# State space layer of a decoder: two states on the two halves of the partitions, sums by 64-column matmuls, and one scan per item in every chunk

## The reference

```python
proj = xc @ W_xproj                      # dt_r (16), Bm (16), Cm (16)
dt = softplus(dt_r @ W_dt + b_dt)        # (b, t, 512)
dA  = exp(dt[..., None] * -exp(A_log))   # (b, t, 512, 16)
dBx = (dt * xc)[..., None] * Bm[:, :, None, :]
h_t = h_{t-1} * dA_t + dBx_t             # from h = 0 for each of 4 sequences
y_t = sum over n of h_t[..., n] * C_t[n]
y = (y + xc * D) * silu(z);  out = x + y @ W_out
```

## Time and profile before

| | |
|---|---|
| median of 3 runs (lowest, highest) | 3203.89 us (3202.26, 3206.14) |
| the profiled execution: its own time, its span | 3204.56 us, 3203.0 us |
| busy over the span | PE 2843.9, DVE 2080.0, POOL 1509.9, ACT 1471.0 us |
| the state space stage | 0 to about 1013 us of the span |
| first scan; first scan of chunk 2 | 40.07 us; 291.29 us |
| mean granted TensorE clock of the whole span | 0.957 |

### The profile page before, as it was taken

The page is one execution under the profiler, slowest core; times in us unless marked ns, Lnnn a source line. Parts: engine busy times, 40 slices in busy tenths (PEclk is TensorE's granted clock), DMA queues, the critical chain, the costliest instruction groups (busy, mean ns, idle before and its releaser), DMA issues. The chain is left out here.

```text
span 3203.0 us, 41427 instructions
## 1 busy us (share of the span) xinstructions
PE 2843.9 (89%) x14210; PEld 1845.6 (58%) x14210; DVE 2080.0 (65%) x3833; ACT 1471.0 (46%) x2768; POOL 1509.9 (47%) x1192
## 2 busy tenths in 40 slices
PE   6898998998977877899999999978877999999998
PEld 2343343343333664555555555546666888888887
DVE  7899999999998654677777777758863222222221
ACT  5667667666763301366666656545541111111111
POOL 5788788888785553133333333256752111111111
PEclk8999999999999788899999999999888999999999
DMA  7135145145140162212322222110115665556662
GB/s 233 51 108 159 46 116 160 35 125 159 34 136 1 41 211 94 81 42 65 81 63 65 58 50 64 50 59 29 50 63 198 200 203 183 181 181 187 205 199 60
DMA packets 283856, 346.32 MB, mean 108 GB/s; under 512 B 85788, under 2 KB 238552, under 8 KB 283592
## 3 DMA queue, kind: packets, MB, share of 16 engines
q1 hardware_dynamic: 260399, 310.17, 31.3%
q0 software_dynamic: 16704, 27.21, 3.6%
q10 hardware_dynamic: 6544, 6.30, 0.7%
HBM read 234.69 MB, written 107.95 MB: 107 GB/s over the span
## 5 line engine op out<-in xcount | busy, mean ns | idle before, releaser
L542 POOL TENSOR_TENSOR mb_drive<-mb_dtx,mb_b_rep 128x1024 f32<-128x1024 f32 x255 | 597.0, 2355 | 179.9 <-DVE mb_pD L439 87.9
L853 PE MATMUL mb_pY<-mb_hc,ident 128*128 128x512 f32 x1024 | 502.9, 616 | 55.9 <-DVE mb_hc L456 55.5
L1981 DVE TENSOR_REDUCE at_nm_of<-at_pS 128x1 f32<-128x128 f32 (+1 forms) x756 | 401.6, 556 | 135.8 <-PE at_pS L1969 75.8
L3153 POOL DMA_INDIRECT out<-et_y,et_to x71 | 112.0, 1577 | 667.0 <-DVE et_y L3207 411.0
L3197 DVE TENSOR_TENSOR et_mT<-et_silu,et_pU 128x512 f32<-128x512 f32 (+1 forms) x160 | 100.3, 628 | 471.2 <-ACT et_silu L3168 471.1
L3168 ACT ACTIVATE et_silu<-et_pG 128x512 f32<-128x512 f32 (+1 forms) x160 | 87.8, 549 | 658.0 <-PE et_pU L3229 658.0
L853 PEld LDWEIGHTS mb_pY<-mb_hc,ident 128*128 128x128 f32 x1024 | 190.3, 195 | 326.9 <-issue 183.3
L1969 PE MATMUL at_pS<-at_kT,at_qT 128*128 128x128 f32 (+1 forms) x756 | 306.3, 407 | 65.3 <-DVE at_nm_of L1981 53.4
L598 ACT ACTIVATE mb_pD<-mb_dt,mb_a_neg 128x512 f32<-128x512 f32 x384 | 259.6, 688 | 157.3 <-DVE mb_hc L456 146.0
L439 DVE TENSOR_TENSOR_SCAN mb_pD<-mb_pD,mb_drive 128x1024 f32<-128x1024 f32 x128 | 292.7, 2287 | 42.9 <-ACT mb_pD L596 40.2
L445 DVE TENSOR_TENSOR_SCAN mb_pD<-mb_pD,mb_carried,mb_drive 128x512 f32<-128x512 f32 x256 | 314.0, 1271 | 6.8 <-ACT mb_pD L598 6.8
(11 more groups left out here) (491 smaller groups left out, 4984.7 us busy)
## 6 DMA issues: line engine op xcount, KB each, us to landing
t_wg<-in_t_wgT SPq DMA_DIRECT2D x40, 1024.0 KB, 6.3
t_wu<-in_t_wuT SPq DMA_DIRECT2D x40, 1024.0 KB, 8.8
t_wd<-in_t_wdT SPq DMA_DIRECT2D x40, 1024.0 KB, 11.3
mb_b_rep<-mb_rows SPq DMA_DIRECT2D x64, 512.0 KB, 5.6
mb_c_rep<-mb_rows SPq DMA_DIRECT2D x64, 512.0 KB, 4.8
t_h_sorted<-blank SPq DMA_DIRECT2D x6, 4160.0 KB, 20.2
t_h_sorted<-blank SPq DMA_DIRECT2D x18, 1170.0 KB, 6.2
t_h_sorted<-blank SPq DMA_DIRECT2D x12, 1040.0 KB, 5.8
```

The costliest lines, as they stand in the source:

```text
L542: nc.gpsimd.tensor_tensor(drive[G % RINGS][:, :, :], dtx[:, m, :].unsqueeze(1).to_broadcast([P, 2, CH]), b_rep[:, 2 * j:2 * j + 2, :], ALU ...
L853: last = nc.tensor.matmul(pY[:, :], K.ident[:, :], hc[G % RINGS][:, k, :], start=False, stop=(j == PAIRS - 1 and k == 1))
L1981: nc.vector.tensor_reduce(nm_of[t % 2][:, w0 // 512, a, qb:qb + 1], score_bank(t, k)[:, 0:w1 - w0], axis=AX.X, op=ALU.max, negate=True).th ...
```

## The change

Two states now lie on the two halves of the partitions (`h`), and two halves of a channel block on the two halves of the free dimension (`k`): `pD[r][h*64 + p, k, t]` is state 2j+h of channel k*64+p. So `b_rep` and `c_rep` have 8 rows to a partition in place of 16 and are loaded by two DMAs of 64 partitions (128 KB) each, for each of b and c. `dt` and `dtx` must be seen by both halves: eight SBUF to SBUF DMAs of 128 KB for each block (`twins`) write them into `dt2` and `dtx2`, which have `TWINS` = 3 slots, and all decays and drives read these. `A_log` is laid out so on the host. The sum over the two states is a matmul with `fold` (two identities of 64 under each other, 64 columns), one for each half of the channels into its 64 partitions of `pY`. In odd chunks there is one scan of 1024 as well: its start is the first carried value, the decay in front of the second half is 0, and ACT adds decay times the second carried value to the first element of the second half's drive. The decays of these first elements come from one more small activation per block (`opening`). `step_sizes` of the next chunk's block 0 comes before drive 29 in place of 31.

```diff
+    TWINS = 3
-        a_neg = sb("a_neg", [P, ME, NST])
+        a_neg = sb("a_neg", [P, ME, 2, PAIRS])
+        fold = sb("fold", [P, HP])
-        b_rep, c_rep = sb("b_rep", [P, NST, CH]), sb("c_rep", [P, NST, CH])
+        dt2, dtx2 = sb("dt2", [P, TWINS, 2, CH]), sb("dtx2", [P, TWINS, 2, CH])
+        b_rep, c_rep = sb("b_rep", [P, PAIRS, CH]), sb("c_rep", [P, PAIRS, CH])
...
+            def twins(ch, m):
+                nth = ch * ME + m
+                q = nth % TWINS
+                for made, to, s_made, s_to, s_used, per in ((dt, dt2, s_dt, s_dt2, s_dec, 2), (dtx, dtx2, s_dtx, s_dtx2, s_drv, 1)):
+                    eng.wait_ge(s_made, nth + 1)
+                    if nth >= TWINS:
+                        eng.wait_ge(s_used, (nth - TWINS + 1) * PAIRS * per)
+                    for k in range(2):
+                        for h in range(2):
+                            eng.dma_start(to[h * HP:(h + 1) * HP, q, k, :], made[k * HP:(k + 1) * HP, m, :]).then_inc(s_to[q], 16)
...
                     if ch > 0:
                         eng.wait_ge(s_drv, last_user + 1)
-                    eng.dma_start(b_rep[:, 2 * j:2 * j + 2, :], rows_dram[ch % 2][2 * j:2 * j + 2, :].partition_broadcast(P)).then_inc(s_b[j], 16)
+                    for h in range(2):
+                        eng.dma_start(b_rep[h * HP:(h + 1) * HP, j, :], rows_dram[ch % 2][2 * j + h, :].partition_broadcast(HP)).then_inc(s_b[j], 16)
                     if ch > 0:
                         eng.wait_ge(s_hc, last_user + 1)
-                    eng.dma_start(c_rep[:, 2 * j:2 * j + 2, :],
-                                  rows_dram[ch % 2][NST + 2 * j:NST + 2 * j + 2, :].partition_broadcast(P)).then_inc(s_c[j], 16)
+                    for h in range(2):
+                        eng.dma_start(c_rep[h * HP:(h + 1) * HP, j, :], rows_dram[ch % 2][NST + 2 * j + h, :].partition_broadcast(HP)).then_inc(s_c[j], 16)
+                    if j == 5:
+                        twins(ch, 0)
                 fill_rows(K, eng, K.h1_sorted, ch, NCH, s_fill)
+                for m in range(1, ME):
+                    twins(ch, m)
...
+        def drive_of(unit, ch, m, j, r):
+            return unit.tensor_tensor(drive[r][:, :, :], dtx2[:, (ch * ME + m) % TWINS, :, :],
+                                      b_rep[:, j, :].unsqueeze(1).to_broadcast([P, 2, CH]), ALU.mult)
...
+                if ch % 2 and G % ITEMS in (0, RINGS):
                     eng.wait_ge(s_keep, ch // 2 * ITEMS + (ITEMS - RINGS if G % ITEMS == 0 else ITEMS))
-                for k in range(2):
-                    eng.wait_ge(s_dec, 2 * G + k + 1)
-                    nc.vector.tensor_tensor_scan(pD[r][:, k, :], pD[r][:, k, :], drive[r][:, k, :],
-                                                 carried[:, m, 2 * j + k:2 * j + k + 1], ALU.mult, ALU.add).then_inc(s_scan, 1)
+                eng.wait_ge(s_dec, 2 * G + 2)
+                both = lambda T: T[r][:, :, :].rearrange("p k t -> p (k t)")
+                before = carried[:, m, j, 0:1] if ch % 2 else 0.0
+                nc.vector.tensor_tensor_scan(both(pD), both(pD), both(drive), before, ALU.mult, ALU.add).then_inc(s_scan, 2)
...
-                    eng.wait_ge(s_dtx, ch * ME + m + 1)
+                    twin_made(eng, s_dtx2, ch * ME + m)
...
-                    if s == 31 and ch + 1 < NCH:
+                    if s == 29 and ch + 1 < NCH:
                         step_sizes(eng, nc.gpsimd, ch + 1, 0)
...
+                nc.scalar.activation(pD[r][:, 1, 1:], step[:, 1:], ACT.Exp, scale=scale)
+                blank = nc.scalar.copy(pD[r][:, 1, 0:1], zeros[:, 0:1])
+                if ch % 2 == 0:
+                    blank.then_inc(s_dec, 1)
+                    return
+                eng.wait_ge(s_opening, ch // 2 * ME + m + 1)
+                eng.wait_ge(s_keep, ch // 2 * ITEMS + G % ITEMS + 1)
+                eng.wait_ge(s_drv, G + 1)
+                nc.scalar.activation(drive[r][:, 1, 0:1], opening[:, m, j:j + 1], ACT.Identity, scale=carried[:, m, j, 1:2],
+                                     bias=drive[r][:, 1, 0:1]).then_inc(s_dec, 1)
...
-                    nc.tensor.matmul(pY[:, :], skip[:, m, :], xc(ch, m), start=True, stop=False)
+                    for k in range(2):
+                        nc.tensor.matmul(pY[k * HP:(k + 1) * HP, :], skip[:, m, k * HP:(k + 1) * HP], xc(ch, m), start=True, stop=False,
+                                         skip_group_check=True)
...
-                    last = nc.tensor.matmul(pY[:, :], K.ident[:, :], hc[G % RINGS][:, k, :], start=False, stop=(j == PAIRS - 1 and k == 1))
+                    last = nc.tensor.matmul(pY[k * HP:(k + 1) * HP, :], fold[:, :], hc[G % RINGS][:, k, :], start=False, stop=(j == PAIRS - 1),
+                                            skip_group_check=True)
```

More of the change, by code:

```diff
@@ L226, in mamba @@
     PAIRS = NST // 2
+    HP = P // 2
+    TWINS = 3
     ITEMS = ME * PAIRS
@@ L288, in mamba @@
             sem(n) for n in ("dec", "drv", "scan", "keep", "hc", "y", "fin", "rows", "fill"))
+        s_dt2, s_dtx2 = [sem(f"dt2_{q}") for q in range(TWINS)], [sem(f"dtx2_{q}") for q in range(TWINS)]
+        s_fold = sem("fold")
+        s_opening = sem("opening")
         s_b = [sem(f"b{j}") for j in range(PAIRS)]
@@ L349, in _, with twin_made @@
             for j in range(PAIRS):
-                eng.wait_ge(s_b[j], 16 * NCH)
-                eng.wait_ge(s_c[j], 16 * NCH)
-        ALL_IN = 16 * 7
+                eng.wait_ge(s_b[j], 32 * NCH)
+                eng.wait_ge(s_c[j], 32 * NCH)
+            for q in range(TWINS):
+                uses = len(range(q, NCH * ME, TWINS))
+                eng.wait_ge(s_dt2[q], 64 * uses)
+                eng.wait_ge(s_dtx2[q], 64 * uses)
+        ALL_IN = 16 * 7
+        def twin_made(eng, s_to, nth):
+            eng.wait_ge(s_to[nth % TWINS], 64 * (nth // TWINS + 1))
+        def drive_of(unit, ch, m, j, r):
+            return unit.tensor_tensor(drive[r][:, :, :], dtx2[:, (ch * ME + m) % TWINS, :, :],
+                                      b_rep[:, j, :].unsqueeze(1).to_broadcast([P, 2, CH]), ALU.mult)
         def normalise(eng, unit, ch):
@@ L426, in first_drive @@
             def first_drive():
[L427 to L430, removed]
+                twin_made(eng, s_dtx2, 0)
+                eng.wait_ge(s_b[0], 32)
+                drive_of(nc.vector, 0, 0, 0, 0).then_inc(s_drv, 1)
             def scans(G):
@@ L470, in _ @@
             nc.vector.memset(K.start.before[:, :], 1.0).then_inc(s_set, 1)
+            nc.vector.tensor_tensor(fold[:, :], K.ident[:, 0:HP], K.ident[:, HP:P], ALU.add).then_inc(s_fold, 1)
             eng.wait_ge(s_cw, 16)
@@ L577, in keep @@
                 eng.wait_ge(s_hc, G + 1)
-                nc.scalar.copy(carried[:, m, 2 * j:2 * j + 2], pD[G % RINGS][:, :, CH - 1]).then_inc(s_keep, 1)
+                nc.scalar.copy(carried[:, m, j, :], pD[G % RINGS][:, :, CH - 1]).then_inc(s_keep, 1)
             def decay(G, k):
@@ L582, in decay @@
                 r = G % RINGS
-                scale = a_neg[:, m, 2 * j + k:2 * j + k + 1]
+                scale = a_neg[:, m, k, j:j + 1]
+                step = dt2[:, (ch * ME + m) % TWINS, k, :]
                 if k == 0:
                     if j == 0:
-                        eng.wait_ge(s_dt, ch * ME + m + 1)
+                        twin_made(eng, s_dt2, ch * ME + m)
                     if G == RINGS - 1:
@@ L593, in decay @@
                             eng.wait_ge(s_keep, back // 2 * ITEMS + (G - RINGS) % ITEMS + 1)
-                if k == 1 and ch % 2 == 0:
-                    nc.scalar.activation(pD[r][:, 1, 1:], dt[:, m, 1:], ACT.Exp, scale=scale)
-                    nc.scalar.copy(pD[r][:, 1, 0:1], zeros[:, 0:1]).then_inc(s_dec, 1)
-                else:
-                    nc.scalar.activation(pD[r][:, k, :], dt[:, m, :], ACT.Exp, scale=scale).then_inc(s_dec, 1)
+                if k == 0:
+                    nc.scalar.activation(pD[r][:, 0, :], step, ACT.Exp, scale=scale).then_inc(s_dec, 1)
+                    if j == 0 and ch % 2:
+                        nc.scalar.activation(opening[:, m, :], a_neg[:, m, 1, :], ACT.Exp,
+                                             scale=dt2[:, (ch * ME + m) % TWINS, 1, 0:1]).then_inc(s_opening, 1)
+                    return
[3 more added lines that the diff above has]
+                    blank.then_inc(s_dec, 1)
+                    return
+                eng.wait_ge(s_opening, ch // 2 * ME + m + 1)
[3 more added lines that the diff above has]
+                                     bias=drive[r][:, 1, 0:1]).then_inc(s_dec, 1)
             def transposed(ch, k):
@@ L749, in _ @@
             projected(0)
-            nc.scalar.activation(a_neg[:, :, :], a_neg[:, :, :], ACT.Exp).then_inc(s_a, 1)
+            nc.scalar.activation(a_neg[:, :, :, :], a_neg[:, :, :, :], ACT.Exp).then_inc(s_a, 1)
             for m in range(2):
```

34 lines of the change are left out of this document (17 added, 17 removed).

## The result

The changed kernel takes 3301.21 us (median of 4 runs, 3296.75 to 3308.99), against 3203.07 us for the kernel before (median of 4, 3202.26 to 3206.14). The ratio is 1.0307, 95% interval 1.0286 to 1.0328: 98 us slower, where 70 were predicted, and inside the range of 3225 to 3314. The profiled execution of the changed kernel has a span of 3298.2 us (3203.0 before).

A forecast was written before the change was run, and what follows sets the result against it. DVE was taken to set the pace, the others having little to spare. Terms -21.5 - 14 + 40 + 12 + 16 + 21 + 12 + 8.5 - 4 = +70 gave 3274 us, range 3225 to 3314.

The forecast's parts named there:

- The copies behind t = 0: Chunk boundary: copies issued only after item 29's weigh ends (t = 0) delay the next chunk's first drive; +40 us, bounds 27 to 49.
- The start: Chunk 0: SP issues 24 half loads before block 0's copies, delaying the first decay and drive; +8.5 us, bounds 4 and 13.
- POOL's lost lead: After the late first drive, POOL runs without a break and drive 3 comes late; +12 us, bounds 0 and 20.
- the fill: Block 1's copies stand behind `fill_rows` on SP, making drive 9 late; +16 us, bounds 0 and 56.
- rival C: The fill holds block 1's copies fully, 56 us in place of 16: 3314 us; chance 0.10.
- Step sizes before drive 29: Chunk end: drive 29 waits behind step sizes that wait for ACT's logarithm; +21 us, bounds 5 and 30.
- both decays: Odd chunks: one scan waits for both of ACT's decays, where the first could start after one; +12 us, bounds 0 and 20.
- The scans: Odd chunks: 128 items go from a period of 3.49 to 3.32 us; -21.5 us.
- The sums: PE's two column groups overlap, cutting DVE's direct and indirect waits for PE; -14 us, bounds 0 and -30.
- B: Only the copies' delay at boundary and start is real, other POOL and ACT lateness hides in it: 3229 us; chance 0.17.
- D: Faster: sums give -30 us and a boundary costs under 5.1 us in all: 3184 us; chance 0.07.
- E: Column groups don't overlap and drains cost PE, so PE gains nothing: 3288 us, or up to 3330; chance 0.04.

The follow-up runs named there:

- the copies moved: Changed kernel with block 0's copies after pair 3 (chunk 0: pair 1), fill behind block 1's copies, step sizes before drive 31: 0.9994 of the kernel before.
- the single moves: Changed kernel with one move each: block 0's copies after pair 3 from chunk 1 on, 1.0181; step sizes before drive 31, 1.0271; fill behind block 1's copies, 1.0274.
- the run with two queues: Kernel with all copies moved, ACT's queue issuing four of block 0's eight copies in chunk 0 instead of SP's: 0.9998 of the kernel before.

## Why the prediction was right, and where it was short

**The copies behind t = 0: right, and too cheap.** The chain at the boundary is the predicted one, step for step, and moving the copies up took it away. It cost 47 us, not 40. The term that was off is the issue spacing: 0.62 to 0.64 us for a half transfer, where I took the 0.47 of two whole ones and not the 0.62 that their whole burst shows. Ten issues make 6.2 us in place of 4.7; the landing, 2.4 us by the median of these transfers, was as assumed. So the drive came 1.5 us later than forecast (8.1, not 6.6). At the boundaries behind odd chunks the wait grew less than that, as DVE too came 1.2 us late, at t = 4.6 in place of 3.4.

**The start: +8.5 predicted, +14.8 measured, outside its bounds of 4 and 13.** The same spacing, 32 issues times 0.17, is 5.4 of the missing 6.3 us. The rest is the first drive: it takes 1.22 us, and the forecast left 0.3 between the landing at 48.3 and the scan.

**POOL's lost lead (12) and the fill (16): 10.3 and 17.1.** Both were read from one chain of POOL and both stood up. That the fill holds up the issuing too (9.98 and 13.21 us for four copies) I had not seen. With block 0's copies early its waits grew to 33 us, near the 38 at scan 29, so rival C's mechanism was nearer than its place in the changed kernel shows.

**Step sizes before drive 29 and both decays: 33 predicted, 38 measured.** The waits were where I put them, 5.44 in even and 5.88 us in odd chunks where it had been 2.40 and 1.2.

**The scans: -21.5 predicted, -13.5 measured.** The step "I take the 2.29 us as they are" failed: with a start value it is 2.348. That alone is 7.5 of the 8 us, and the run without the start value shows it. The 3.32 us period that was to be a sign in odd chunks came as 3.38.

**The scan's merger as a whole.** By my terms it was worth -21.5 + 12 = -9.5. It is worth nothing with the copies moved, nothing in the changed kernel, and it costs 12 us in the kernel before: a second scan of 512 was covering ACT's second decay, and I counted that cover at too little. Why it pays 27 us of waits in the kernel before and 16 with the copies moved is not shown; the two differ in the layout and in the width of the sums.

**The sums: -14 predicted; the wide ones cost 24 and 18 us.** Right sign, inside the bounds, too small. But both were measured with one scan in odd chunks. With two scans no run has wide sums in this layout. An estimate, from one profile of each kernel: with one scan and wide sums the new layout ends its last weigh 6.8 us after the old one (1035.0 and 1028.2). Added to the 1013.4 of the kernel before, that is 1020.2 with two scans, and the narrow sums bring it to 1016.5, which is a gain of 4 us. So most of what narrow sums gain may be what one scan costs without them. Whether the changes of tiling mode drain PE can't be told apart here; the sums gain all the same, as the four of an item take 337.3/256 = 1.32 us of PE in place of 1.96. (The row of 32 columns that I read at 128x128 is 77x128.)

**The rivals.** B said that the later delays hide in the first. They did not while the first stood: all of the groups are in the account. They did in part when one was removed, which is why by the last weigh the single moves gave 80 us and all together 98. D needed the sums to be worth 30 and a boundary under 5.1 us; it cost 6.8. E is excluded by the cost of the wide sums; its upper end was also too low, as 0.3 us on 256 items are 77 us, not 42.

So the forecast of 3274 came out 27 us low mostly from sizes. By the table the start is off by 6.3 us, the boundaries by 7.4, scans 3 and 9 by -0.6, the waits around scan 29 by 5, the scans by 8 and the rest by 8. That is 34, of which the shorter later stages hid 9 by no merit of the forecast. Without them it would be 3310, still inside the range. One thing was missed outright, the queue held at issue; the price of the start value was put at nothing for want of a row.

## What to carry to other kernels

Look for the place in an in-order queue, before the cost of the transfer: copies whose data was long ready stood here behind a load that waits for the end of the chunk, and behind a fill, and the step sizes stood ahead of two drives, where they waited for a logarithm. Moving these gave back the 100 us. A merged instruction waits for the union of what its parts waited for, so price the cover that the first part gave the second's producer, not only its overhead. Read a spacing from a whole burst, not from its first pair. And price moves together: each one alone hands part of its gain to the next delay in line.

## What the runs showed of the hardware

- Two transfers to 64 partitions each don't cost what one to 128 does. In the burst at the start, 16 whole loads of B and C (512 KB) went out 0.62 us apart in the mean (0.39 to 1.07), halves (128 KB) 0.64, so a pair takes about twice as long to issue. The Trainium skill (DMA: Bandwidth & Descriptors, Rules for kernel authors) says that transfers to disjoint partition halves serialise, and one of 128 partitions should be used; the run with two queues agrees, as its eight copies, to either half, landed 0.58 us apart though they were issued 0.3 apart.
- A queue can be held at issue by a large transfer ahead of it: four copies took 9.98 and 13.21 us to go out behind the 4160 KB fill, and the same four 2.40 ahead of it.
- A scan of 1024 columns takes 0.06 us longer with a start value read from memory than with a constant (2346 against 2288 ns).
- The granted clock went with the width of the sums more than with the stalls: 0.88 with narrow sums and no boundary stall, 0.97 with wide ones, in the same chunk (shares of the full 2.4 GHz; over such a stretch a mean of the two levels, 1.2 and 2.4). With the stalls of the changed kernel it was 0.86 (narrow) and 0.93 (wide). PE was busy for 94.55 of 120 us in the one and 110.15 of 123 in the other. The kernel was faster at the lower clock; what the clock itself costs no run separates.
